# Three small attentions of a decoder: score units in pairs, causal masks last, row maxima handed on earlier

## The reference, cut to what matters

```python
scores = jnp.einsum('bqhd,bkhd->bhqk', q, k) * scale
causal = jnp.tril(jnp.ones((s, s), dtype=bool))
scores = jnp.where(causal[None, None], scores, jnp.finfo(scores.dtype).min)
probs = jax.nn.softmax(scores, axis=-1)
out = jnp.einsum('bhqk,bkhd->bqhd', probs, v).reshape(b, s, H)
```

## Time and profile before

| | |
|---|---|
| median of three runs | 3243.72 us |
| the profiled execution, own time | 3246.41 us |
| its span | 3244.8 us |
| TensorE busy | 2318.6 us, 71% of the span |
| VectorE, ScalarE, GpSimd busy | 1846.5, 1086.2, 781.9 us |
| granted TensorE clock, mean over the span | 0.787 |
| first, second, third call of the function | about 382, 124 and 121 us |

### The profile page before, as it was taken

The page is one execution under the profiler, slowest core; times in us unless marked ns, Lnnn a source line. Parts: engine busy times, 40 slices in busy tenths (PEclk is TensorE's granted clock), DMA queues, the critical chain, the costliest instruction groups (busy, mean ns, idle before and its releaser), DMA issues. The chain is left out here.

```text
span 3244.8 us, 36291 instructions
## 1 busy us (share of the span) xinstructions
PE 2318.6 (71%) x13182; PEld 1520.0 (47%) x13182; DVE 1846.5 (57%) x3528; ACT 1086.2 (33%) x2191; POOL 781.9 (24%) x765
## 2 busy tenths in 40 slices
PE   4477873399996588875413678887899968785738
PEld 1233322156664577762301344445788845544424
DVE  6677876634345455534687734443455554495377
ACT  1334441344443244431022233333343434202422
POOL 0122220045553566551243000000222210000020
PEclk7655556699997799997755678888899987796879
DMA  2000000000000344430000000002000000000000
GB/s 94 0 1 1 1 1 18 13 11 19 19 13 25 109 150 159 148 128 30 4 35 0 32 3 3 3 3 85 1 1 1 1 1 2 15 25 1 2 31 13
DMA packets 31104, 97.64 MB, mean 30 GB/s; under 512 B 3920, under 2 KB 16720, under 8 KB 29648
## 3 DMA queue, kind: packets, MB, share of 16 engines
q1 hardware_dynamic: 29392, 91.12, 8.3%
q0 software_dynamic: 1536, 4.20, 0.4%
HBM read 83.31 MB, written 11.01 MB: 29 GB/s over the span
## 5 line engine op out<-in xcount | busy, mean ns | idle before, releaser
L1716 POOL TENSOR_SCALAR l0f_probs<-l0f_probs,l0f_tot 128x128 f32<-128x128 f32 (+1 forms) x256 | 190.9, 767 | 241.6 <-DVE l0f_tot L1682 241.6
L1285 DVE TENSOR_REDUCE l2a_a_max<-ps 128x6 f32<-128x768 f32 x128 | 120.5, 956 | 118.6 <-PE ps L1142 117.8
L1931 PE MATMUL ps<-l0f_xh,l0f_wh 128*128 128x256 f32 x480 | 147.6, 307 | 41.5 <-issue 31.7
L2044 POOL TENSOR_TENSOR l0f_wl<-l0f_raw,l0f_wh 128x1024 fp32r<-128x1024 f32 x60 | 141.8, 2375 | 32.0 <-ACT l0f_wh L1968 32.0
L1932 PE MATMUL ps<-l0f_xl,l0f_wh 128*128 128x256 f32 x480 | 139.0, 290 | 0.0
L1933 PE MATMUL ps<-l0f_xh,l0f_wl 128*128 128x256 f32 x480 | 138.9, 289 | 0.0
L1623 ACT ACTIVATE l0f_probs<-ps,l0f_neg 128x128 f32<-128x128 f32 (+1 forms) x256 | 104.5, 425 | 92.8 <-DVE l0f_neg L1672 92.8
L2868 POOL TENSOR_TENSOR l2x_probs<-l2x_probs,l2x_rc 128x512 f32<-128x512 f32 x64 | 66.6, 1041 | 265.0 <-DVE l2x_rc L2783 265.0
L612 POOL TENSOR_TENSOR l0x_y<-l0x_y,l0x_hc 128x512 f32<-128x512 f32 x64 | 79.8, 1268 | 202.9 <-DVE l0x_hc L603 202.9
L1931 PEld LDWEIGHTS ps<-l0f_xh,l0f_wh 128*128 128x128 f32 x480 | 95.1, 198 | 54.3 <-issue 42.3
L1541 PE MATMUL ps<-l0f_xT,l0f_slab 128*128 128x512 f32 x192 | 95.5, 625 | 33.0 <-DMA l0f_slab<-in_g_l0f 32.9
(11 more groups left out here) (779 smaller groups left out, 6110.0 us busy)
## 6 DMA issues: line engine op xcount, KB each, us to landing
l0f_raw<-in_e_l0f SPq DMA_DIRECT2D x60, 768.0 KB, 4.4
scratch_rows<-zero SPq DMA_DIRECT2D x1, 3840.0 KB, 18.9
l0f_xb<-scratch_rows SPq DMA_DIRECT2D x15, 256.0 KB, 4.8
scratch_results<-l0f_yb SPq DMA_DIRECT2D x15, 256.0 KB, 5.0
l0f_slab<-in_g_l0f SPq DMA_DIRECT2D x8, 448.0 KB, 3.9
l1f_raw<-in_w_l1f SPq DMA_DIRECT2D x1, 3072.0 KB, 10.3
l2f_ew<-in_e_l2f SPq DMA_DIRECT2D x8, 384.0 KB, 3.0
l3f_raw<-in_w_l3f SPq DMA_DIRECT2D x1, 2438.0 KB, 8.7
```

Of the source, the lines that this page charges most:

```text
L1285: dve.tensor_reduce(M[:, 2 * half:2 * half + 2, j, :], src.rearrange("p a (c n) -> p a c n", c=NB_), AX.X, ALU.max).then_inc(*unit_max.tick())
L1716: last = pool.tensor_scalar(pr[:, u % 3, a, r], pr[:, u % 3, a, r], tot[:, u % 3, qt, a:a + 1], None, ALU.mult)
L1931: pe.matmul(out, hi, xh[:, j % 2, c, :], start=c == 0, stop=False)
L2044: pool.tensor_tensor(wl[:, n % 2, :], raw[:, n % 4, 0:1024], wh[:, n % 2, :].bitcast(F32), ALU.subtract).then_inc(*w_lo.tick())
```

## The change

Four things are changed in `small_attention`:

- A new `pair` does two units of a step together. It waits for both ring slots first; then come all matmuls of the first query tile, all of the second, and then the masks of the one unit and of the other. In the first call the four heads of a pair lie in four different row groups; in the other two calls the pair's units share the same two groups.
- `units_at` gives two units to each of the first steps: steps 0 to 7 in the first call (before, 16 units over steps 0 to 9), 0 to 3 in the second (as before), 0 to 3 in the third (before, 8 over steps 0 to 5).
- `turn_rows`, with its work on VectorE and the DMAs behind it, moves from step `NC - 2` to step `LAST`: from 10 to 8, stays at 4, from 6 to 4.
- Within a step weigh and back now come ahead of the units and of `turn_rows`, and VectorE normalises ahead of the maxima.

The probabilities' tile is laid out in another order of its axes, so the exponential writes in pieces of 256 elements; the matmuls that read it read the same 256 or 128 elements in a row. Sizes and counts of matmuls, masks, exponentials, copies and DMAs are unchanged.

```diff
+    LAST, LAG = max(NU // 2, NC - 4), 1
@@ units_at
-        return [u for u in range(NU) if u * (NC - 2) // NU == s]
+        return [u for u in range(NU) if u // 2 * LAST // (NU // 2) == s]
@@ the list uses
+        uses += [("weigh", O, 0) for O in octet_at(n, LAG)] + [("back", O, 0) for O in octet_at(n, LAG + 1)]
         if 0 <= it - 1 < NB2:
-            uses += [("unit", it - 1, u) for u in units_at(s)] + ([("rows", it - 1, 0)] if s == NC - 2 else [])
-        uses += [("weigh", O, 0) for O in octet_at(n, 1)] + [("back", O, 0) for O in octet_at(n, 2)]
+            uses += [("unit", it - 1, u) for u in units_at(s)] + ([("rows", it - 1, 0)] if s == LAST else [])
@@ tiles
-        PT, oT4, rinv = sb("probs", [P, 2, 2, 2, 4, S]), sb("oT4", [P, 2, 2, S]), sb("rinv", [P, 2, 2, 2, 4])
+        PT, oT4, rinv = sb("probs", [P, 2, 2, 4, 2, S]), sb("oT4", [P, 2, 2, S]), sb("rinv", [P, 2, 2, 2, 4])
@@ at_pe
-            def unit(b, u):
-                z, (j, half) = b % 3, hs.units[u]
-                banks = ring("unit", b, u)
-                if u == 0:
+            def pair(b, us):
+                z = b % 3
+                if us[0] == 0:
                     pe.wait_ge(*t_sb(NT_ * (b + 1)))
-                pe.wait_ge(*ring_free("unit", b, u))
+                for u in us:
+                    pe.wait_ge(*ring_free("unit", b, u))
                 for qt in range(2):
                     w = P if causal and qt == 0 else S
                     at = qt * (P if causal else S)
-                    for a in range(2):
-                        r = hs.rows(2 * half + a, K)
-                        last = pe.matmul(banks[:, a, at:at + w], QT[z][r, j, qt * P:(qt + 1) * P], KT[z][r, hs.kj(j), 0:w],
-                                         start=qt == 0, stop=not causal and qt == 1)
+                    for u in us:
+                        j, half = hs.units[u]
+                        for a in range(2):
+                            r = hs.rows(2 * half + a, K)
+                            last = pe.matmul(ring("unit", b, u)[:, a, at:at + w], QT[z][r, j, qt * P:(qt + 1) * P], KT[z][r, hs.kj(j), 0:w],
+                                             start=qt == 0, stop=not causal and qt == 1)
+                        if qt == 1 and not causal:
+                            last.then_inc(*unit_ps.tick())
                 if causal:
-                    for a in range(2):
-                        diagonal = banks[:, a, :].rearrange("p (q n) -> p q n", n=S)[:, :, 0:P]
-                        last = pe.matmul(diagonal, k.identb, k.mask_qk.unsqueeze(1).to_broadcast([P, 2, P]), start=False, stop=True)
-                last.then_inc(*unit_ps.tick())
+                    for u in us:
+                        for a in range(2):
+                            diagonal = ring("unit", b, u)[:, a, :].rearrange("p (q n) -> p q n", n=S)[:, :, 0:P]
+                            last = pe.matmul(diagonal, k.identb, k.mask_qk.unsqueeze(1).to_broadcast([P, 2, P]), start=False, stop=True)
+                        last.then_inc(*unit_ps.tick())
...
+                for O in octet_at(n, LAG):
+                    weigh(O)
+                for O in octet_at(n, LAG + 1):
+                    back(O)
                 if 0 <= it - 1 < NB2:
-                    for u in units_at(s):
-                        unit(it - 1, u)
-                    if s == NC - 2:
+                    us = units_at(s)
+                    for i in range(0, len(us), 2):
+                        pair(it - 1, us[i:i + 2])
+                    if s == LAST:
                         turn_rows(it - 1)
-                for O in octet_at(n, 1):
-                    weigh(O)
-                for O in octet_at(n, 2):
-                    back(O)
@@ at_act
-                    act.activation(PT[:, O % 2, :, kt, 2 * p:2 * p + 2, :].rearrange("p a j s -> p a (j s)"), banks, ACT.Exp, scale=scale).then_inc(*weighed.tick())
+                    act.activation(PT[:, O % 2, kt, 2 * p:2 * p + 2, :, :].rearrange("p j a s -> p a j s"), banks.rearrange("p a (j s) -> p a j s", s=S), ACT.Exp, scale=scale).then_inc(*weighed.tick())
```

30 lines of the change are left out of this document (16 added, 14 removed).

## The result

The changed kernel takes 3289.28 us (median of four runs, 3283.36 to 3294.26) against 3245.12 us (3240.46 to 3247.18) for the kernel before: a ratio of 1.0142 [1.0129, 1.0156]. It is slower by 1.4%, 44 us. The forecast was 3251 us with a range of 3227 to 3283; the result lies above both. Its span is 3283.6.

A forecast was written before the change was run, and what follows sets the result against it. TensorE at the full clock was taken as the bound; calls of -9, +14 and +2 us summed to +7 on 3246.4, so 3253.4, or 3251 us from the median. Own range 3240 to 3266, overall range 3227 to 3283.

The forecast's parts named there:

- The pair's matmuls: First call, TensorE: four heads run as fast as two, a pair costs 0.98 us not 1.50; 4.2 us less per batch.
- The third rival: Four heads do not run at once, a pair costs up to 1.50 us: 3272 us in all; chance 0.05.
- The short waits: First call: TensorE waits around pairs, backs and rows for ring slots and copies, 6.9 us per batch instead of 2.9.
- The rows earlier, the DMA wait: Wait for the maxima's DMAs per batch: 4.8 to 3.3 us in first call, 2.5 in second, nearly gone in third.
- The slow clock in the first call: Per first-call batch: 3.0 us instead of 4.4 behind the DMA wait, plus 1.8 for one more slow stretch.
- The first pass: Units before the first score: pairs waiting out two maxima cost about 3 us, counted in the second call.
- Second call: Rows behind the weigh, pairs' waits and a lower clock in the two middle batches: plus 14 us.
- Third call: DMA wait nearly goes, batch stays at 23.5 to 24 us, TensorE less busy in four steps: plus 2 us.
- Nothing for the rest: Exponential's output in pieces of 256, DMAs, VectorE's and GpSimd's counts: no effect on the time.
- The first, no further fall of the clock: Rival: the calls give -22, +9 + 2 and -2, so the change is faster, 3231 us; chance 0.25.
- the second: Rival: the clock falls twice in each batch or stays down, +34, 3278 us; chance 0.2.
- F: Experiments' theory: clock falls in the scores and units at a batch's start, gaps or not; full-array constant matmuls there hold it.

The follow-up runs named there:

- e5: The changed kernel with the rows' transposes, joining and splitting of the maxima put at the head of their step: 3276.87 us, ratio 1.0103.
- e1: The changed kernel with its pairs undone, units issued one by one; early rows and new order kept: 3250.09 us, ratio 1.0024.
- e3: The kernel before with only the earlier steps for units and rows; units one by one, old order: 3234.23 us, ratio 0.9968.
- e11: The changed kernel, a pair's second unit waiting for its own slot only after the first unit's matmuls, masks still last: 3280.06 us, ratio 1.0102.
- e14: The changed kernel with row DMAs merged into two and five constant matmuls before the second score of first-call batches but the first: 3247.62 us, ratio 1.0017.
- e12: e3 with constant matmuls in the row waits (13 first call, 2 third) and five before the second score of first-call batches: 3211.99 us, ratio 0.9909.
- e15: e3 with row DMAs merged into two and five constant matmuls before the second score of first-call batches but the first: 3183.19 us, ratio 0.9821.
- e9: e1 with constant matmuls filling the DMA waits, 13 in the first call and 2 in the third: 3238.95 us, ratio 0.9989.
- e16: e15 with the five constant matmuls in all three calls and in the first scored batch too: 3201.97 us, ratio 0.9875.
- e6: The kernel before with constant matmuls ahead of the wait for the rows, 18 in the first call and 15 in the third: 3247.77 us, ratio 1.0002.

## Why the prediction was wrong, point by point

**The pair's matmuls: right.** 0.97 against 0.98: the scores of four heads take the 0.43 us that those of two did. The third rival, four heads not at once, is out.

**The short waits: nearly right.** Plain 1.03 (forecast 1.0), behind a weigh 0.79 (0.75), behind a back 0.85 (0.7), ahead of the rows 0.92 (0.7). The last was put down to ScalarE's copy of the turned stack; it is the joining of the maxima L1296, behind the normalising. By the window of the batch idle is 44.9 - 34.35 = 10.55; less the DMA wait, 7.2 (forecast 6.9).

**The rows earlier, the DMA wait: right.** 3.31 against 3.3 in the first call, 2.48 against 2.5 in the second, one wait left in the third.

**The slow clock in the first call: the step that failed.** The premise was that the clock is at 1.00 between the DMA waits, read from one batch; the batch after it, of 47.4 us, had a second slow stretch (2081.5), and I passed over it. I took 3.0 us per batch behind the DMA wait and 1.8 for one more stretch of half a length, in each batch the same. The stretch behind the wait did not end with the first weigh, as it had before: it ran through the pair, the score and half the turn behind it (11.2 us). By the groups, a score costs 0.5 more in it, the pair at 2017.82 0.6, the weigh 1.3, the next pair 0.7, the wide score 0.7 and the turn 0.2: 4.0. The stretch at 2045.3 adds 1.5 (the weigh 1.3, the score ahead of it 0.2). That is 5.5 instead of 4.8, and such a batch took 44.9 and not 43.3; 0.3 more are short waits, and the rest, some 0.6, is in work that I had counted too low. In three of the seven gaps there was a third slow stretch, and they took 47.3 to 47.4, 2.4 more. The seven gaps rose from 314 to 320 us where minus 9 had been forecast: 15 us, about half of what the forecast missed.

**The first pass: left out of the first call.** I costed the pairs' wait for two maxima ahead of the first score in the second call (about 3) and not in the first. There most pairs wait 1.58 us at the low clock, and the pass grew from 41.4 to 46.4: 5 of the 20 us by which the first call was missed.

**Second call:** +18 against +14. The wait for the rows was right (2.48), and e5 shows what the rows' place is worth: ahead of the weigh they give back 10.8. The low clock was taken too small: slow time went from 51 to 75, some 10 us at 0.43, where 5 had been forecast.

**Third call:** +7.6 against +2. "The batch stays at 23.5 to 24" fell: the DMA waits went from 17.3 to 5.3, but the pairs and turns took much of it, 5.9 and 5.0 us, and the slow time rose from 78 to 96. Groups of the third call before:

```profile
L1137 PE MATMUL ps<-l3a_a_KT,l3a_a_QT 48*128 48x256 f32 x128 | 20.5, 424 | 10.6 <-DVE l3a_a_max L1285 7.1 <-ACT l3a_a_QT L1236 3.2 <-DVE l3a_o L1310 0.2
L1169 PE MATMUL ps<-l3a_a_QT,l3a_a_KT 50*128 50x512 f32 x64 | 18.7, 588 | 17.9 <-DMA l3a_a_QT<-l3a_a_mrow 17.3 <-ACT l3a_a_probs L1249 0.6
L1123 PE MATMUL ps<-kf,l3a_a_sq 128*128 128x128 f32 x64 | 13.7, 389 | 0.9 <-DVE l3a_a_sq L1277 0.7 <-DVE l3a_a_max L1285 0.2
```

and after:

```profile
L1175 PE MATMUL ps<-l3a_a_QT,l3a_a_KT 50*128 50x512 f32 x64 | 18.6, 578 | 6.7 <-DMA l3a_a_QT<-l3a_a_mrow 5.3 <-ACT l3a_a_probs L1256 1.5
L1140 PE MATMUL ps<-l3a_a_KT,l3a_a_QT 48*128 48x256 f32 x128 | 18.0, 420 | 16.5 <-DVE l3a_a_max L1292 6.8 <-ACT l3a_a_QT L1243 4.8 <-DVE l3a_o L1317 2.0
L1124 PE MATMUL ps<-kf,l3a_a_sq 128*128 128x128 f32 x64 | 15.4, 425 | 5.9 <-DVE l3a_a_max L1292 5.2 <-DVE l3a_a_sq L1284 0.7
```

With the units one by one (e1) the call takes 112.7: the pairs are worth 13.7 here, and without them it is 6 us shorter than before.

**Nothing for the rest.** The new layout of the probabilities is in all four parts, in e3 too, which is the faster for all that; by itself it was not tried. Nothing in the rows speaks of a price: the exponential takes 1.02 us before and after, and a weigh at the full clock 1.51.

**The rivals.** The first, no further fall of the clock, had the batch right but for the clock, and the clock decided. What happened is the second, which I gave 0.2: two slow stretches in each batch of the first call, and a third in four of the seven gaps, the last and shorter one among them. Its numbers by call were +13, +17 and +4, which is 3280.4 on the execution's own time; measured was 3285.1. I had seen what speaks for it, the third call's clock of 0.68 at 67% busy and the 63% of the plain steps. I mixed these to 80% in the mean and set that beside the 82% of the earlier trace rows. The rule of the Trainium skill that I had named for it ("TensorE: Matmul & The Clock Gate", A second HAM failure mode) is borne out in part: the clock swings here, and the fall at 2045.3 comes with no long wait ahead, behind pairs that wait 0.8 to 1.0 us each. But that the brief waits are its cause is not shown: the kernel before has such a fall without them (2081.5), and e11 has fewer waits and a lower clock.

## What stays open

What exactly lets the clock fall inside the batches of the change. It is not idle time alone (e11 has half of it in the first call and more slow time) and not the run of scores and units alone at the place where the fills stand (e14). F is borne out where there are no pairs (e12, e15) and did not forecast e9, e14 or e16. The three patterns of a batch, 44.6, 44.9 and 47.3 us, come from the same instructions. e1, e3, e6, e9 and e14 have spreads of 21 to 30 us between their ten runs, where the kernel before has 14 to 19 in 13 or 19; one profile of each doesn't show why. The number 0.43 is from two pairs of kernels (0.43 and 0.42) and one call. Whether pairs would pay with more ring slots, so that they need not wait for both, was not tried: the ring and the second score already take banks 0 to 7.

## What to carry to other kernels

Work that is merged to save an engine's time must not need more free buffers at once than the pieces did: here 0.5 us saved per pair was answered by 0.8 to 1.0 us of waiting for a free slot. On TensorE price a new wait twice, once as idle time and once as slow clock (0.43 us per slow microsecond here), and price it by the stretch it stands in, not by the mean busy share of a batch. Before moving work to cover a transfer, look at the transfer: issuing eight small ones took 5.4 us, issuing the same as two took 1.1, and this was worth four times what moving the rows earlier gave.

## What the runs showed that was not expected

- The granted clock fell with TensorE busy for all of the 2.2 us ahead of the fall and for 4.87 of the 5.8 before them (e6), and in the kernel before with 12.7 of the last 13.6 us busy, in runs of matmuls on 24 to 26 rows with masks on all 128 between them; with 1.2 us of full-array matmuls put among them it stayed at 1.00 for whole batches (e12).
- Less idle time can be slower: e11 has 47 us less of it in the first call and takes 12 us more, 27 us of work and some 30 for the clock having come in its place.
- Four matmuls on four row groups cost what two cost: a pair has 0.43 us of scores for four heads, as a unit has for two (2041.17 to 2041.60, and the earlier trace rows).
- One transfer may write partitions at a step of 32 or 64, and its issue on SyncE costs 0.54 us, against 0.67 for one of a quarter of the size in the first call.
